# Key-value sums of a linear attention computed per image in column tiles, turned back by products with an identity, and the first loads and all engine orders rearranged

## The chip, the cores and the metric

The program runs on one core of one Trainium2 chip. The metric is device microseconds (us) of one execution. Each kernel is a single launch that takes the inputs of the reference, as float32, from HBM and writes the output back to HBM. Everything is computed in float32.

## The reference

The input is 8 images of 48 channels and 48 x 48 pixels. Two layers follow each other. The first is window attention (8 x 8 windows, 4 heads), a gated 1x1 convolution, a 3 x 3 convolution and a residual. The second is a depthwise block with linear attention and an MLP. The part that the change rewrites is the linear attention of the second layer:

```python
qk = t @ qk_w.T + qk_b                       # t: (b, n, 48) tokens, n = 2304
q = elu(qk[..., :c]) + 1.0
k = elu(qk[..., c:]) + 1.0
q_rope, k_rope = rope(q), rope(k)            # pairs of channels turned by the position
z = 1.0 / (einsum('bhnd,bhmd->bhnm', qh, k.mean(n)) + 1e-6)
kv = einsum('bhnd,bhne->bhde', k_rope * scale, v * scale)     # 8x8 per head, summed over n
attn = einsum('bhnd,bhde->bhne', q_rope, kv) * z
```

In the first layer the queries and keys are `x @ qkv_w.T + qkv_b`, and their biases are also touched.

## The kernel before, in words

The 8 images are worked on as 4 pairs (i = 0..3). Each pair is cut into 3 chunks of 16 image rows (n = 0..2), 768 pixels of each image. A tile has the 48 channels of one image on partitions 0 to 47 and those of the other on 64 to 111.

A job such as `kv.2.1` is one step of pair 2, chunk 1. Each engine has a table (`PE_ORDER`, `ACT_ORDER`, `DVE_ORDER`, `POOL_ORDER`, `SP_ORDER`) that lists its jobs in the order in which it issues them, and it never leaves that order. Jobs wait on semaphores. A PE job also names one of four PSUM slots (`@0` to `@3`); the slot must have been read by its previous user. Pair i+1's first layer is interleaved with pair i's second layer, so that only the second layer of pair 3 stands alone at the end.

Jobs that the prediction speaks of, first layer: `q1`, `k1` (queries, keys; L646), `qb` (DVE) and `kx` (ACT, L953) read them out, `xw` (ACT, L944) regroups pixels into windows, `v` (values, L703), `sc0..3` (scores, L718), `sb0..3` (DVE: add the bias, take the maximum, L1186 and L1190), `su` (POOL: subtract it), `ex` (ACT: exp, L974), `tr0..3` (transposes, L729), `pt` (ACT), `sm` (sums, L739), `av`, `pj`, `w1a`, `w1b`, `g`, and `cv` (the 3 x 3 convolution, 36 matmuls, L656 with `G`).

Second layer: `d0` (depthwise convolution as 36 matmuls, L656 with `ZP`), `ip`, `c10..c18` (DVE: nine taps of a depthwise convolution, L1230 and L1234), `ts`, `q`, `kt`, `vt` (queries, keys, values; L814, L804, L821), `c20..c28` (DVE: nine taps, L1245 and L1248), `kr`, `qs`, `qc` (POOL: rotations), and then the steps that change:

- `kv` (L829, L835): for each of the 8 token tiles of a chunk (98 rows: 96 tokens and a gap of two), keys (98 x 96, both images) are the weights, and a column of ones or the values (98 x 96) stream. The rotated keys come as two tiles, `KC` (times cosine) and `KS` (times sine). The result has keys of both images against values of both images; only the two diagonal blocks are used.
- `ks` (DVE, L1273, L1275) adds the three chunks of a pair in `kv_sum`.
- `kp` (L844 to L847) brings `kv_sum` into the layout with 64 partitions per image with matrices `wide_sb` (an identity and a swap of neighbouring channels); DVE `kp` scales it and cuts it to the heads (L1281, L1283), into `kv_sb` and `km_sb`.
- `kk` (L853) multiplies `kv_sb` by the swap matrix; DVE `kk` copies that to `kv2_sb` (L1289).
- `dn` (L862: the denominators, needs `kp`), `at` (L875: needs `kp`, `kk`, `qs`, `qc`), `az`, `am` (DVE), `ym` (POOL, L1393), `op` (L637), `oz` (DVE), `d3` (a second depthwise convolution, L656), `xc2`, `va2`, `f10..f12`, `f2`.

Before the first job, DVE and POOL clear tiles; SP and ACT issue the loads of weights. PE starts with a wait for all 30 loads of the group `loaded_a` (`pe.wait_ge(loaded_a, N_A * 16)`, L898). The last loads, 49 of `loaded_b`, are issued ahead of SP's order, whose first entry is `lx.0.2`, the load of the third chunk of pair 0.

Of the kernel before, what the change touches and what calls it, by code (L numbers as in the profile page):

```python
# [26 lines left out]
CH = 3  # L27
# [42 lines left out]
    cv.0.1@3 k1.1.1@0 cv.0.2@2 q1.1.1@1 d0.0.0@0 d0.0.1@1 xc.0.0@0 sc0.1.1@2 xc.0.1@1 tr1.1.0@3 va.0.0@0 va.0.1@1  # L70
    d0.0.2@3 tr2.1.0@2 ip.0.0@0 sc1.1.1@3 ip.0.1@1 v.1.0@0 tr3.1.0@1 sc2.1.1@3 sc3.1.1@0 xc.0.2@2 va.0.2@2 sm.1.0@1
    tr0.1.1@3 ip.0.2@2 q1.1.2@1 tr1.1.1@3 k1.1.2@2 ac.0.0@0 v.1.1@3 sc0.1.2@1 av.1.0@2 tr2.1.1@0 tr3.1.1@1 sc1.1.2@3
    ac.0.1@2 vt.0.0@0 sc2.1.2@1 pj.1.0@2 sm.1.1@0 q.0.0@3 tr0.1.2@2 sc3.1.2@0 w1b.1.0@1 kt.0.0@2 av.1.1@0 tr1.1.2@3
    k1.2.0@1 q1.2.0@2 pj.1.1@0 q.0.1@3 kt.0.1@2 v.1.2@0 tr3.1.2@3 tr2.1.2@2 sc0.2.0@1 w1a.1.0@3 sm.1.2@2 sc1.2.0@0
    kv.0.0@1 sc2.2.0@2 tr0.2.0@0 vt.0.1@3 av.1.2@0 sc3.2.0@3 q1.2.1@2 w1b.1.1@1 kt.0.2@0 pj.1.2@2 v.2.0@1 tr1.2.0@3
    k1.2.1@2 kv.0.1@0 q.0.2@3 vt.0.2@2 sc0.2.1@1 ac.0.2@0 kv.0.2@2 tr2.2.0@3 kp.0.0@2 sc1.2.1@3 tr3.2.0@0 dn.0.0@2
    dn.0.1@1 w1a.1.1@0 sm.2.0@3 kk.0.0@0 sc2.2.1@2 at.0.0@0 dn.0.2@1 w1b.1.2@3 cv.1.0@2 at.0.1@1 tr0.2.1@0 w1a.1.2@2
    av.2.0@3 sc3.2.1@0 cv.1.1@2 op.0.0@0 v.2.1@2 tr1.2.1@3 op.0.1@1 q1.2.2@0 pj.2.0@2 k1.2.2@3 d3.0.0@1 at.0.2@0
    tr2.2.1@1 xc2.0.0@3 sc0.2.2@2 tr3.2.1@1 va2.0.0@3 w1b.2.0@0 cv.1.2@1 f10.0.0@0 op.0.2@2 f11.0.0@3 f12.0.0@0
# [1443 lines left out]
```

## Time and profile before

| | |
|---|---|
| median of 3 runs | 820.52 us (816.24 to 821.81) |
| profiled execution, its own time | 821.09 us |
| span of the profiled execution | 819.3 us |
| PE busy | 700.7 us, 86% |
| DVE busy | 536.2 us, 65% |
| ACT busy | 428.2 us, 52% |
| POOL busy | 299.6 us, 37% |
| mean granted TensorE clock | 0.906 |

The span runs from the first to the last instruction; the execution's own time is 1.8 us longer. Busy times overlap between the engines, so they don't add up to the span. Float32 matmuls appear as two records each in the trace, so that 8 matmuls read x16.

### The profile page before, as it was taken

Reading aid. Unit: us, or ns where it says so; the run is one execution under the profiler, and the core shown is the slowest. Engines: PE = TensorE matmul, PEld = TensorE weight load, DVE = VectorE, ACT = ScalarE, POOL = GpSimd, SP = SyncE. Lnnn points to the kernel's source line nnn. Section 1 sums busy time; section 2 is a strip of 40 time slices with the busy share of each in tenths; the row PEclk is TensorE's granted clock in tenths of the full one; section 3 lists DMA queues with packets and bytes.
Section 4 is the critical chain, followed back from the end, with each engine's and each line's share of the span. In section 5 each row is a group of like instructions: output and inputs, shape, how many; then the busy total and the mean of one; then the engine's idle time right before and its main releaser. Section 6 shows DMA issues by size and latency. Waiting matters only on the chain. (4 is left out here: it accounts for less than half of the span.)

```text
span 819.3 us, 20532 instructions
## 1 busy us (share of the span) xinstructions
PE 700.7 (86%) x8964; PEld 416.1 (51%) x8964; DVE 536.2 (65%) x569; ACT 428.2 (52%) x521; POOL 299.6 (37%) x197
## 2 busy tenths in 40 slices
PE   1979989689896999989898999879789997686895
...
PEclk9999999889898999999889999876799998595799
...
GB/s 60 54 45 32 16 47 31 44 2 30 31 2 16 16 17 69 51 30 32 1 16 2 2 61 45 60 1 2 1 1 3 31 61 43 1 2 0 1 2 44
DMA packets 20395, 20.57 MB, mean 25 GB/s; under 512 B 9712, under 2 KB 19056, under 8 KB 20306
## 3 DMA queue, kind: packets, MB, share of 16 engines
...
q10 hardware_dynamic: 2080, 0.29, 0.2%
...
## 5 line engine op out<-in xcount | busy, mean ns | idle before, releaser
L656 PE MATMUL ps<-ZP,wdw 48*64 48x384 f32 x1728 | 148.3, 495 | 7.5 <-DVE ZP L1303 5.1
L1374 POOL TENSOR_TENSOR SC<-SC,mx 128x768 f32<-128x768 f32 x48 | 82.5, 1720 | 197.1 <-DVE mx L1190 196.9
L1248 DVE SCALAR_TENSOR_TENSOR CT<-TP,vec_sb,CT 112x768 f32<-112x768 f32 x96 | 146.8, 1539 | 1.8
L1234 DVE SCALAR_TENSOR_TENSOR QS<-ZP,vec_sb,QS 112x768 f32<-112x768 f32 x96 | 113.8, 1192 | 2.3
L656 PEld LDWEIGHTS ps<-ZP,wdw 48*64 48x64 f32 x1728 | 74.3, 136 | 78.0 <-issue 37.2
L1186 DVE TENSOR_TENSOR SC<-ps,bias_sb 128x768 f32<-128x768 f32 x48 | 45.7, 952 | 65.9 <-PE ps L718 32.0
L656 PE MATMUL ps<-G,w_sb 48*64 48x384 f32 x864 | 76.2, 501 | 6.5 <-ACT G L1007 6.2
L1220 DVE TENSOR_TENSOR LV<-LV,XB 112x768 f32<-112x768 f32 x24 | 25.9, 1081 | 72.5 <-ACT LV L1039 72.5
L935 ACT ACT_TABLE_LOAD x56 | 71.8, 1283 | 1.0
L656 PEld LDWEIGHTS ps<-G,w_sb 48*64 48x64 f32 x864 | 38.9, 138 | 41.1 <-issue 16.3
L729 PE MATMUL ps<-ident_sb,SC 128*128 128x128 f32 x288 | 48.1, 316 | 5.8 <-ACT AR L1051 2.6
L982 ACT ACTIVATE PT<-ps 128x768 f32<-128x768 f32 x48 | 38.1, 807 | 25.2 <-issue 12.7
L1345 POOL TENSOR_TENSOR KC<-KK,rope_th_sb 98x384 f32<-98x384 f32 x12 | 17.3, 1440 | 90.2 <-DVE KK L1254 90.1
L646 PE MATMUL ps<-XR,wt_sb 49*64 49x384 f32 x192 | 26.9, 644 | 26.4 <-DMA bv_sb<-in_vec_dram 18.0
L729 PEld LDWEIGHTS ps<-ident_sb,SC 128*128 128x128 f32 x288 | 37.4, 161 | 22.1 <-issue 19.3
L974 ACT ACTIVATE SC<-SC 128x768 f32<-128x768 f32 x48 | 39.7, 838 | 16.0 <-POOL SC L1374 15.8
L718 PE MATMUL ps<-kx,qw 32*64 32x128 f32 x1152 | 45.4, 302 | 1.9 <-DVE qw L1177 1.0
L1381 POOL TENSOR_TENSOR YF<-X1T,YF 112x768 f32<-112x768 f32 x12 | 21.3, 1778 | 69.7 <-ACT YF L1016 69.7
L1190 DVE TENSOR_REDUCE mx<-SC 128x12 f32<-128x768 f32 x48 | 45.7, 953 | 1.7
L1393 POOL TENSOR_TENSOR CT<-CT,AR 112x768 f32<-112x768 f32 x12 | 22.4, 1871 | 62.0 <-DVE CT L1298 62.0
L718 PEld LDWEIGHTS ps<-kx,qw 32*64 32x64 f32 x1152 | 34.1, 146 | 16.4 <-issue 11.6
L1090 ACT ACTIVATE QH<-ps,fc1b 128x768 f32<-128x768 f32 x36 | 30.5, 899 | 18.8 <-PE ps L646 18.7
...
## 6 DMA issues: line engine op xcount, KB each, us to landing
...
XR<-in_x_dram SPq DMA_DIRECT2D x24, 144.0 KB, 2.7
X1T<-in_x_dram SPq DMA_DIRECT2D x24, 144.0 KB, 2.9
...
out_dram<-XB SPq DMA_DIRECT2D x24, 144.0 KB, 2.3
...
```

Source lines behind the costliest of these rows:

```text
L656: mm = pe.matmul(slot(job)[half(c, HALF), r * BANK:r * BANK + SPX], w[half(r), tap * HALF:(tap + 1) * HALF], shifted(t, d * CROWS + c * WI ...
L718: mm = pe.matmul(slot(job)[half(c, HALF), p * BANK + wp * 128:p * BANK + (wp + 1) * 128] .rearrange("p (h y x) -> p h y x", h=2, y=WIN), q ...
L729: mm = pe.transpose(slot(job)[:, j * 128:(j + 1) * 128], SC[q % NSC][:, j * 128:(j + 1) * 128], ident_sb[:, :])
L935: act.preload_act_table_set(TABLE[name, i, n])
L974: act.activation(SC[q % NSC], SC[q % NSC], ACT.Exp).then_inc(exp_ready, 1)
L982: act.activation(PT[q % NPT], slot(job)[:, 0:CPX], ACT.Copy).then_inc(free(job), 2)
L1090: act.activation(pairs(HB[:, m, :]), two(job, 128), ACT.Gelu, bias=fc1b2[:, m:m + 1])\
L1186: dve.tensor_tensor(sc, two(job, 128).rearrange("p b (j m) -> p b j m", m=TOK), bias_sb[:, :].unsqueeze(1).unsqueeze(1).broadcast_to([128, ...
L1190: dve.tensor_reduce(mx[:, (q % NSC) * 12:(q % NSC) * 12 + 12], SC[q % NSC].rearrange("p (j m) -> p j m", m=TOK), AX.X, ALU.max)\
L1234: dve.scalar_tensor_tensor(out=rows16(T0[n]), in0=win, scalar=wt, in1=rows16(T0[n]), op0=ALU.mult, op1=ALU.add).then_inc(dwc_step, 1)
L1248: dve.scalar_tensor_tensor(out=ct, in0=win, scalar=wt, in1=ct, op0=ALU.mult, op1=ALU.add).then_inc(lepe_step, 1)
L1374: pool.tensor_tensor(sc, sc, bc_last(mx[:, (q % NSC) * 12:(q % NSC) * 12 + 12], TOK), ALU.subtract).then_inc(sub_ready, 1)
```

## The change

What is computed stays the same. The parts are:

1. **Key-value sums.** In `kv` the values are now the weights and the rotated keys stream, one image at a time: 98 x 48 weights, 48 streamed columns, image 0 into PSUM partitions 0 to 47 and image 1 into 64 to 111. The products of the two images are issued in turn, and there is nothing of image 0 against image 1 any more. A chunk has 16 + 32 matmuls where it had 8 + 16, each with half the weight columns and half the streamed columns (the means stream 2 as before).
2. **Turning back.** `ks` adds 112 x 96 and 112 x 2. With the third chunk, four more small DVE operations (112 x 24) combine the cosine and sine sums into `kv_turn`. `kp` transposes it by products with an identity: 12 matmuls of 48 rows and 64 columns. DVE `kp` has three operations where it had four. `kk` is gone from PE and DVE, and so are `swap_sb`, `wide_sb` and their ten loads.
3. **First-layer biases.** The query and key biases are no longer a 49th row of the weights (eight loads of 24 elements); they are added when DVE and ACT read the products out, from `vq_sb` and `kb_sb`.
4. **First loads.** The four loads of query and key weights come first on SP and have a semaphore of their own (`loaded_q`), for which PE waits at its start. The other 18 of `loaded_a` are waited for by `s1`, `v.0.0`, the first `tr`, and by DVE, which makes `kb_sb`. `lx.0.2` is issued before the last weights. `w2` has its own semaphore. Clearing of `vx`, `YF` and `XA` moves from DVE to POOL.
5. **Orders.** All five tables are new.

```diff
 PE_ORDER = """
-    k1.0.0@0 q1.0.0@1 s1.0.0@2 sc0.0.0@0 sc1.0.0@2 sc2.0.0@1 v.0.0@3 sc3.0.0@0 k1.0.1@2 q1.0.1@3 tr0.0.0@1 sc0.0.1@2
...
+    k1.0.0@0 q1.0.0@1 s1.0.0@2 v.0.0@3 sc0.0.0@0 sc2.0.0@2 sc1.0.0@3 sc3.0.0@1 k1.0.1@0 q1.0.1@3 tr0.0.0@0 tr1.0.0@2
...
-        N_A, N_B, N_W = 30, 49, 6
+        N_A, N_B, N_W, N_Q, N_C = 18, 37, 6, 4, 2
...
+            sp.wait_ge(zeroed, 1)
+            load(0, 0)
...
+            run("lx", 0, 2)
             load_turned(0, 1)
             load_turned(0, 2)
...
                 elif name in ("q1", "k1"):
                     pe.wait_ge(x_loaded[n], i * 32 + 32)
-                    turned(job, w4("q" if name == "q1" else "k", slice(0, K1)), XR[(i * CH + n) % 2], C + 1)
+                    turned(job, w4("q" if name == "q1" else "k", slice(0, K1)), XR[(i * CH + n) % 2])
...
                     for t in range(CT_):
-                        pe.matmul(ps[0:R, R:R + 2], KK[n % 2][:, t * R:(t + 1) * R], ones2,
-                                  start=(t == 0), stop=(t == CT_ - 1))
+                        for b in range(2):
+                            at = t * R + b * C
+                            pe.matmul(ps[half(b), BANK:BANK + 2], KK[n % 2][:, at:at + C], ones2,
+                                      start=(t == 0), stop=(t == CT_ - 1))
                     wait_read(pe, ("vt", i, n))
                     pe.wait_ge(kcs_ready, KR_COUNT["kr", i, n] * 4)
-                    for src, at in ((KC, 0), (KS, BANK)):
-                        for t in range(CT_):
-                            mm = pe.matmul(ps[0:R, at:at + R], src[n % 2][:, t * R:(t + 1) * R],
-                                           VT[:, t * R:(t + 1) * R], start=(t == 0), stop=(t == CT_ - 1))
+                    for t in range(CT_):
+                        for src, to in ((KC, 0), (KS, C)):
+                            for b in range(2):
+                                at = t * R + b * C
+                                mm = pe.matmul(ps[half(b), to:to + C], VT[:, at:at + C], src[n % 2][:, at:at + C],
+                                               start=(t == 0 and src is KC), stop=(t == CT_ - 1 and src is KS))
...
-                elif name == "kk":
-                    wait_read(pe, ("kp", i, 0))
-                    wait_slot(pe, job)
-                    pe.matmul(slot(job)[0:RG, 0:2 * HALF], swap_sb[:, :], kv_sb[:, :], start=True, stop=True)\
-                        .then_inc(fill(job), 1)
...
-            pe.wait_ge(loaded_a, N_A * 16)
+            pe.wait_ge(loaded_q, N_Q * 16)
...
+                    if n == CH - 1:
+                        wait_read(dve, job)
+                        even = lambda t, at: t[:, at:at + C].rearrange("p (c u) -> p u c", u=2)[:, 0]
+                        odd = lambda t, at: t[:, at:at + C].rearrange("p (c u) -> p u c", u=2)[:, 1]
+                        dve.tensor_tensor(even(kv_turn, 0), even(kv_sum, 0), odd(kv_sum, C), ALU.subtract)
+                        dve.tensor_tensor(odd(kv_turn, 0), odd(kv_sum, 0), even(kv_sum, C), ALU.add)
+                        dve.tensor_tensor(even(kv_turn, HALF), odd(kv_sum, 0), even(kv_sum, C), ALU.add)
+                        dve.tensor_tensor(odd(kv_turn, HALF), odd(kv_sum, C), even(kv_sum, 0), ALU.subtract)\
+                           .then_inc(kv_turned, 1)
```

**The head on SP.** The first loads as SP issues them, before:

```order
L500 DMA XR<-in_x_dram 48x768 x2
L512 DMA wt_sb<-in_wsq_dram 48x2x24 x4
L512 DMA wt_sb<-in_vec_dram 1x24x1 x8
L512 DMA wproj_sb<-in_wproj_dram 24x48
L512 DMA bv_sb<-in_vec_dram 24x1
```

(three more pairs of `wproj_sb` and `bv_sb` follow, and then the second `XR`.) With the change:

```order
L501 DMA wt_sb<-in_wsq_dram 48x2x24 x4
L498 DMA XR<-in_x_dram 48x768 x2
L516 DMA vq_sb<-in_vec_dram 24x20 x4
L498 DMA XR<-in_x_dram 48x768 x2
L516 DMA wproj_sb<-in_wproj_dram 24x48 x4
L512 DMA X1T<-in_x_dram 48x2x384 x2
L507 DMA wt_sb<-in_wsq_dram 48x2x48 x2
L507 DMA wt_sb<-in_vec_dram 1x48x1 x4
L498 DMA XR<-in_x_dram 48x768 x2
```

The eight loads of bias elements are gone, and the third `XR` load (`lx.0.2`), which stood behind all weights, is now ahead of the last `X1T` loads.

**PE at the end of pair 2's attention**, where `G` marks the convolutions `cv.3.n` of pair 3 and `ZP` the convolutions `d3.2.n` of pair 2. Before, from the last output product of pair 2 (`op.2.2`, L637) to the first convolution of pair 3's second layer (`d0.3.0`, the last row):

```order
L637 MATMUL ps<-CT,wsq_sb 112x384 x2
L646 MATMUL ps<-LV,wln_sb 64x384 x4
L656 MATMUL ps<-ZP,wdw 64x384 x36
L646 MATMUL ps<-LV,wfc_sb 64x384 x8
L646 MATMUL ps<-XB,wln_sb 64x384 x4
L656 MATMUL ps<-ZP,wdw 64x384 x36
L646 MATMUL ps<-LV,wfc_sb 64x384 x4
L646 MATMUL ps<-LV,wln_sb 64x384 x4
L646 MATMUL ps<-XB,wln_sb 64x384 x4
L656 MATMUL ps<-G,w_sb 64x384 x36
L646 MATMUL ps<-LV,wln_sb 64x384 x4
L892 MATMUL ps<-QH,wfc_sb 64x384 x12
```

With the change, the stretch between the first `dn` of pair 2 (L871) and that output product has all three `G` convolutions:

```order
L871 MATMUL ps<-QH,km_sb 64x384 x4
L658 MATMUL ps<-G,w_sb 64x384 x36
L871 MATMUL ps<-QH,km_sb 64x384 x4
L884 MATMUL ps<-QH,kv_sb 64x384 x4
L884 MATMUL ps<-QS,kv_sb 64x384 x4
L658 MATMUL ps<-G,w_sb 64x384 x36
L871 MATMUL ps<-QH,km_sb 64x384 x4
L884 MATMUL ps<-QH,kv_sb 64x384 x4
L884 MATMUL ps<-QS,kv_sb 64x384 x4
L639 MATMUL ps<-CT,wsq_sb 112x384 x2
L658 MATMUL ps<-G,w_sb 64x384 x36
L639 MATMUL ps<-CT,wsq_sb 112x384 x2
```

So `cv.3.2` no longer stands between pair 2's output product and `d0.3.0`.

**DVE at the start of pair 2's taps.** `SC` and `mx` are the last softmax step of pair 3 (`sb3.3.2`), `QS` the taps `c1x.2.n`, `CT` the taps `c2x.2.n`. With the change:

```order
L1196 TENSOR_TENSOR SC<-ps,bias_sb 128x768
L1200 TENSOR_REDUCE mx<-SC 128x12
L1240 TENSOR_SCALAR QS<-ZP,vec_sb 112x768
L1244 SCALAR_TENSOR_TENSOR QS<-ZP,vec_sb,QS 112x768 x2
L1207 TENSOR_TENSOR NI<-ps,NI 128x768
L1244 SCALAR_TENSOR_TENSOR QS<-ZP,vec_sb,QS 112x768
```

Before, that softmax step stood behind all 27 `QS` taps and the first `CT` taps. Now it stands ahead of them; the other first-layer steps of pair 3 (`nm`, `x1`, `g`) stay between the taps.

## Rows read from the trace of the kernel before

**Rows 1.** The page: PE's busy time, and the granted clock in 40 slices.
```profile
PE 700.7 (86%) x8964; PEld 416.1 (51%) x8964; DVE 536.2 (65%) x569; ACT 428.2 (52%) x521; POOL 299.6 (37%) x197
...
PEclk9999999889898999999889999876799998595799
```
**Rows 2.** Stretches: from:to, us, busy PE, PEld, DVE, ACT, POOL (instructions), granted clock, DMA, GB/s.
```profile
55.00:519.00 464.00, 428.78 (x6142) 255.06 (x6142) 312.94 (x337) 272.59 (x340) 175.65 (x103) 0.94 0.09 26
519.00:627.00 108.00, 89.39 (x1014) 57.56 (x1010) 92.00 (x88) 51.26 (x63) 47.12 (x28) 0.81 0.04 12
627.00:658.00 31.00, 30.36 (x360) 16.00 (x355) 4.82 (x5) 16.53 (x18) 4.68 (x3) 1.00 0.08 21
...
697.00:753.00 56.00, 39.24 (x294) 30.32 (x294) 54.32 (x54) 26.26 (x27) 34.10 (x20) 0.68 0.00 1
```
**Rows 3.** Waits of PE: us in total, times, longest.
```profile
PE ps L656 <- ACT G L1007: 6.2, 1, 6.2
```
**Rows 4.** Timeline of the head: start, us, engine, line, operation, [idle before]; q: DMA issue.
```profile
0.74 0.31 POOL L1319 MEMSET wt_sb<- 113x256 f32 x1 [0.29 <-POOLq L1513]
...
5.27 0.43 ACTq L908 DMA_DIRECT2D masks_sb<-in_masks_dram  x1
5.29 1.87 SPq L512 DMA_DIRECT2D wt_sb<-in_wsq_dram  x4
...
7.20 6.19 SPq L512 DMA_DIRECT2D wt_sb<-in_vec_dram  x8
...
12.72 0.73 ACTq L908 DMA_DIRECT2D wide_sb<-in_const_dram  x1
...
18.02 2.84 PE L646 MATMUL ps<-XR,wt_sb 49*64 49x384 f32 x16 [18.02 <-DMA bv_sb<-in_vec_dram]
...
19.65 1.69 ACT L953 ACTIVATE kx<-ps,hmask_sb 128x768 f32<-128x768 f32 x2 [4.89 <-PE ps L646]
...
21.23 0.93 ACT L944 ACTIVATE XW<-XR 112x384 f32<-112x384 f32 x2
...
29.24 1.28 ACT L935 ACT_TABLE_LOAD   x1
...
32.06 1.54 PE L729 MATMUL ps<-ident_sb,SC 128*128 128x128 f32 x6
...
48.60 2.84 PE L646 MATMUL ps<-XR,wt_sb 49*64 49x384 f32 x16 [4.64 <-DMA XR<-in_x_dram]
...
52.84 2.53 PE L739 MATMUL ps<-PT,ones_sb 128*32 128x384 f32 x16
```
**Rows 5.** The page's DMA issues: count, KB, median us from issue to landing.
```profile
XR<-in_x_dram SPq DMA_DIRECT2D x24, 144.0 KB, 2.7
```
**Rows 6.** Timeline of PE: one chunk of `kv` and what follows it, pair 0.
```profile
196.63 1.52 PE L829 MATMUL ps<-masks_sb,KK 98*96 98x2 f32 x16
198.01 1.58 PE L835 MATMUL ps<-VT,KC 98*96 98x96 f32 x16
...
200.88 0.89 PE L718 MATMUL ps<-kx,qw 32*64 32x128 f32 x24
```
**Rows 7.** Timeline of PE: the value products of pair 0, chunk 1.
```profile
60.08 1.60 PE L703 MATMUL ps<-wv_sb,XW 112*64 112x48 f32 x48
```
**Rows 8.** Timeline of DVE: two of its steps between the taps of pair 2.
```profile
570.91 0.96 DVE L1186 TENSOR_TENSOR SC<-ps,bias_sb 128x768 f32<-128x768 f32 x1 [0.89 <-PE ps L718]
...
594.63 0.29 DVE L1289 COPY kv_sb<-ps 112x128 f32<-112x128 f32 x1 [2.52 <-PE ps L853]
```
**Rows 9.** Timeline of PE: the last convolution of pair 3's first layer.
```profile
647.39 6.02 PE L656 MATMUL ps<-G,w_sb 48*64 48x384 f32 x72
```
**Rows 10.** Timeline of DVE in the last pair: six taps in a row.
```profile
727.98 11.74 DVE L1248 SCALAR_TENSOR_TENSOR CT<-TP,vec_sb,CT 112x768 f32<-112x768 f32 x6
```
**Rows 11.** Timeline of PE in the last pair: `kp` and `dn`.
```profile
740.94 0.58 PE L844 MATMUL ps<-kv_sum,wide_sb 96*112 96x48 f32 x2 [5.74 <-DVE kv_sum L1275]
...
744.13 1.56 PE L862 MATMUL ps<-QH,km_sb 48*64 48x384 f32 x8 [0.82 <-DVE kv_sb L1283]
```

More of the change, by code:

```diff
@@ L70 @@
[L70 to L79, printed above, removed]
@@ new lines @@
+    g.1.2 sb0.2.1 c25.0.1 sb1.2.1 ks.0.2 sb2.2.1 kp.0.0 sb3.2.1 qb.2.2 c24.0.0 c25.0.0 c26.0.1 c26.0.0 nm.2.0 c27.0.0
+    az.0.0 c28.0.0 az.0.1 c27.0.1 am.0.0 sb0.2.2 c28.0.1 x1.2.0 am.0.1 c20.0.2 c21.0.2 oz.0.0 c22.0.2 oz.0.1 c23.0.2
+    c24.0.2 c25.0.2 c26.0.2 c27.0.2 az.0.2 c28.0.2 am.0.2 g.2.0 oz.0.2 sb1.2.2 yn2.0.0 sb2.2.2 sb3.2.2 nm.2.1 yn2.0.1
+    o.0.0 qb.3.0 yn2.0.2 sb0.3.0 sb1.3.0 o.0.1 yn.1.0 o.0.2 sb2.3.0 yn.1.1 x1.2.1 c10.1.0 c11.1.0 c12.1.0 sb3.3.0
+    c13.1.0 qb.3.1 c14.1.0 yn.1.2 c15.1.0 nm.2.2 c16.1.0 g.2.1 c17.1.0 c10.1.1 c18.1.0 c10.1.2 c11.1.1 x1.2.2 c12.1.1
@@ new lines @@
+    c11.1.2 c13.1.1 c12.1.2 qo.1.0 c13.1.2 c14.1.1 ko.1.0 c15.1.1 c14.1.2 c16.1.1 c15.1.2 c17.1.1 c16.1.2 c18.1.1
+    c17.1.2 sb0.3.1 c18.1.2 ks.1.0 sb1.3.1 c20.1.0 ko.1.1 c20.1.1 g.2.2 c21.1.1 c21.1.0 c22.1.1 ko.1.2 c22.1.0 c23.1.1
+    c23.1.0 qo.1.1 c24.1.0 ks.1.1 c25.1.0 ks.1.2 qo.1.2 c26.1.0 nm.3.0 kp.1.0 c27.1.0 c24.1.1 c28.1.0 c25.1.1 sb2.3.1
+    az.1.0 am.1.0 c26.1.1 x1.3.0 c27.1.1 az.1.1 c28.1.1 am.1.1 oz.1.0 c20.1.2 c21.1.2 c22.1.2 oz.1.1 c23.1.2 az.1.2
+    c24.1.2 c25.1.2 c26.1.2 c27.1.2 c28.1.2 am.1.2 sb3.3.1 oz.1.2 qb.3.2 yn2.1.0 g.3.0 sb0.3.2 sb1.3.2 yn2.1.1 o.1.0
@@ L575, in _ @@
                 for m in range(2):
-                    load_a(wt4_g[half(b), m, :, 0:hh_],
+                    load_q(wt4_g[half(b), m, :, 0:hh_],
                            wsq3[img, m, img].rearrange("r (g c) -> r g c", g=2))
-            bias_row(load_a, "bq", "q")
-            bias_row(load_a, "bk", "k")
+            sp.wait_ge(zeroed, 1)
+            load(0, 0)
+            sp.wait_ge(setup_pool, 2)
+            for b in range(2):
+                for g in range(2):
+                    rows = slice(b * HALF + g * QUAD, b * HALF + g * QUAD + hh_)
+                    load_a(vq_sb[rows, :], vec[g * hh_:(g + 1) * hh_, 0:VI["bv"] + 1])
+            sp.wait_ge(zeroed, 2)
+            load(0, 1)
             for b in range(2):
@@ L917, in _ @@
                     load_a(hmask_sb[row:row + C // 2, :], masks[g * (C // 2):(g + 1) * (C // 2), 2 + 2 * g:4 + 2 * g])
[L918 to L920 removed]
+            for b in range(2):
+                load_a(wv_sb[half(b), :], wsq[b * C:(b + 1) * C, 2 * R:3 * R])
+            load_a(bias_sb[:, :], bias)
+            load_a(ident_sb[:, :], ident)
+            for b in range(2):
+                load_a(vec_sb[half(b), :], vec[b * C:(b + 1) * C, :])
+            act.wait_ge(setup_pool, 3)
             load_b(masks_sb[:, :], masks)
@@ L1324, in _ @@
             op_.then_inc(setup_pool, 1)
+            pool.memset(vx, 0.0).then_inc(setup_pool, 1)
+            for j in range(2):
+                op_ = pool.memset(YF[j], 0.0)
+            op_.then_inc(setup_pool, 1)
+            pool.memset(XA[:, :], 0.0)
             pool.memset(ZP[:, :, :], 0.0)
```

348 lines of the change are left out of this document (173 added, 175 removed).

## The prediction

> **What bounds the kernel now.** I read the page's busy times first. PE is busy 700.7 us of 819.3, more than any other engine, at a granted clock that is mostly full and falls in a few slices [rows 1]. Then the busy time by stretch [rows 2] shows three regimes. From 55 to 519 us PE is busy 92% (428.8 of 464) at clock 0.94: here PE work removed is time removed. From 519 to 627, pair 2's taps, DVE is busy 92.0 of 108 us, PE 89.4 at clock 0.81: DVE's order sets the pace, and PE waits in between. From 627 to 658 PE alone works (30.4 of 31, DVE 4.8). From 697 to 753, in the lone pair 3, DVE is busy 54.3 of 56 and PE's clock is 0.68. Ahead of all that lies a head in which PE stands 18.02 us for the first loads and once more 4.64 us for a third `XR` load [rows 4]. So a change is worth its PE time in the first regime, its DVE time in the second and last, and its start in the head.
>
> **The sum, against the profiled execution's own 821.1 us.**
>
> *Head.* POOL's first clearing ends at 0.74 + 0.31 = 1.05. The four weight loads (1.87) then end their issue at 3.0, the `XR` load (as the six of pair 0, 0.9) at 3.9, and it lands 2.7 later [rows 4, 5]: PE starts near 6.8, where it started at 18.02. Eight bias loads of 6.19 us are gone. PE can't use all of it. ACT issues 5 loads after its first ten, not 13; those 13 took 5.27 to 13.45, 0.63 each, and the ten took from 0.74 to 5.27, so ACT is free at 1.4 + 4.5 + 3.2 = 9.1 (the 1.4 is POOL's second group of clearings, an estimate from its first). Then follow a table load 1.28, `xw` 0.93 and `kx` 1.69 [rows 4]: `v` starts at 11.3. PE is at its low clock here (a transpose takes 1.54), so I give `v` twice the 1.60 of its full-clock row, less overlap, 2.9, four score steps 1.5 each, like the transpose, and the next key product half of 2.84: to 21.6 [rows 4, 7]. ACT runs the second `kx` *before* the first `ex`, so 1.7, a table load of 1.3 and one activation (half of `kx`'s pair, 0.85) pass before the first transpose: about 25.5, against 32.06 [rows 4]. That is 6.5 less. From there to the first `sm`, PE took 20.8 us, 4.64 of them the wait for `XR`, which now stands ahead of the late weights. The same PE work lies in between. So `sm.0.0` comes at 41.7, not 52.84, 11.1 less. Of this I take **-10.2**, because DVE runs `sb1` before `sb2` where PE runs `sc2` first, which can cost one of these steps. Bounds: -6.5 if the `XR` wait comes back, -15 if ACT's late loads don't hold it.
>
> *Key-value sums.* A chunk took from 196.63 to 200.88, 4.25 us for 48 records, 88 ns each, with 2 streamed columns as with 96 [rows 6]. Now there are 96 records in two column halves. The nearest row is `v`: weights of 112 x 64 in two column halves, 48 columns streamed, 48 records in 1.60 us, 33 ns each [rows 7]. 96 x 33 ns = 3.2 us, 1.07 less per chunk. `kp` and `kk` had 14 records (2.4 us at the low clock in the last pair up to `dn` with their DVE part 3.2 [rows 11], about half of the PE part at full clock, 1.2, and 0.6 for `kk`); 24 records at 33 ns are 0.8, 1.0 less. In the PE-bound regime there are six chunks and two `kp`: 6 x 1.07 + 2 x 1.0 = **-8.4**. Pair 2's three chunks lie beside DVE's taps, pair 3's under 54.3 us of DVE in 56: nothing there for themselves. The bounds: 88 ns per record as before would make a chunk 8.4 us, +4.2; half of `v`'s time would make it 1.6, -2.7.
>
> The Trainium skill (TensorE: Matmul & The Clock Gate, Back-to-back issue gap) has an issue floor of about 25 ns for small matmuls; an estimate by that page is 96 x 25 = 2.4 us per chunk, which would make the sum 5 us lower. No run here shows that floor for these shapes, and the row for `v` is above it.
>
> *Pair 2 beside the taps.* `sb3.3.2` (0.96 + 0.95) leaves the taps' stretch for the PE-bound one before it. The `kk` copy goes, and the 2.52 us for which DVE stood before it [rows 8]; 0.5 us of new small DVE operations come (estimate: four of about 0.12). DVE had 16 us idle in this stretch, so some of this may only move: **-4.2**, between 0 and -12.
>
> *`cv.3.2`.* It was one of the jobs of 627 to 658, where PE alone works: 6.02 us [rows 9]. It moves in among pair 2's `at` and `op`, where PE idles 18.6 of 108 us. The work between `op.2.2` and `d0.3.0` falls by its 5.8 us of pace: **-5.8**. Price if the cover is gone: it delays `at.2.1` or `op.2.1` by up to 5.8, and the gain is nil.
>
> *Last pair.* `ks.3.2` and `kp` come after 9 `CT` taps instead of 11, at 11.74 / 6 = 1.96 us each [rows 10], while `kv.3.2` is ready: -3.9. `kp` to `dn` took 3.2 us [rows 11]; four DVE operations of some 0.1, 24 short records and three DVE operations give 2.2: -1.0. But DVE now runs tap `c28.3.2` after `az.3.2`, on the chain to the last `op`: +1.0. Together **-3.9**, between 0 and -8. What is late next there is POOL, whose `qc.3.0` and `qc.3.1` start with `dn`.
>
> *Orders.* In pairs 0 and 1, the 6.2 us wait of `cv.1.1` for its edges [rows 3] should go: 24 us of PE work now lie between `w1a.1.2` and it. Against that, `pj.2.2` now stands right behind `av.2.2`, `w1b.1.1` right behind `pj.1.1`, and `vt` right ahead of `kv` in pair 1. I put this at **0**. PE idles 35 us in 55 to 519 [rows 2], so new waits could bring +17 (half as much again), or -12 (a third less).
>
> Sum: -10.2 - 8.4 - 4.2 - 5.8 - 3.9 = -32.5, so 788.6 for the execution's own time. The median of the three runs shown is 0.6 us under that of the profiled one: **788 us**.
>
> **The rivals.**
>
> *A. The order's own waits (805 us).* Each term above assumes that no other wait takes its place. With +17 from 55 to 519 us the sum is 805.6 and the median 805. For it: DVE is already busy 313 of 464 us there, and `sb3.3.2` and parts of pair 3's softmax are now in it. Against it: the distances in PE work between producer and consumer are mostly as long as before.
>
> *B. The head is swallowed (798 us).* If the first convolutions wait for weights or the `YF` path, the 10.2 is lost. Against it: PE is busy nearly throughout from 55 us on, and the late weights are issued earlier too.
>
> *C. The column halves don't run side by side (830 us, slower).* The place is `kv`: both halves use all 98 rows, and stream different columns. If each record costs 88 ns as before, a chunk costs 8.4 us: +4.2 on each of six chunks (25), instead of -6.4, and about +8 in pairs 2 and 3 where PE has room for the rest: 788.6 + 6.4 + 25 + 8 = 828, and with `kp` 830. It decides from 44 ns per record on: above that `kv` is dearer than before. Against it: `v` has the same form and runs at 33 ns [rows 7].
>
> The Trainium skill (TensorE: Matmul & The Clock Gate, What overlaps and what doesn't) says that a weight load overlaps running matmuls only when its row group differs. By that rule the two halves, which share all rows, would come one after the other. The row for `v` disagrees, since its halves share 112 rows.
>
> *D. More than the sum (776 us).* With three convolutions in the waits of pair 2, PE's clock, 0.81 there, stays full, and 12 of DVE's 16 idle us go.
>
> **How the numbers follow.** Chances: forecast 0.58, A 0.20, B 0.07, C 0.05, D 0.10. The predicted time is the forecast's. The range is 774 to 808: it takes in the forecast, B, D and most of A, and leaves out C and A's far end. About 1% (8 us) is what a measurement can tell from no change. Faster by more than that (under 812) are all cases but C and a tail of A: 0.89. Within 1%: 0.06. Slower: 0.05.
>
> **What would show it.** PE's first record near 7 us, the first transpose near 26, the first `sm` near 42. A `kv` chunk of 96 records in 3.2 us at full clock. `d0.3.0` 27 to 30 us earlier than 657.7, and its distance to the end 3 to 5 us shorter. No wait of 6 us for `G`. Wrong it would be if a chunk takes over 4.2 us, if PE idles clearly more than 35 us between the first `sm` and pair 2's taps, or if DVE idles as long as before among pair 2's taps.

## The result and the profile after

The changed kernel took **796.75 us** (median of 4 runs, 794.74 to 800.78) against 820.52 before: a ratio of 0.9725, 95% interval 0.9668 to 0.9782. A second set of runs gave 799.63 and 0.9711 (0.9645 to 0.9777). The profiled execution took 800.78, the second set's 799.63. Now and then a kernel runs at a lower clock and takes 1.5% or more longer; medians and ranges in this document count such runs, ratios and their intervals leave them out. The forecast was 788, the range 774 to 808: faster as forecast, but 9 us short of it.

Page of the kernel after, busy times and granted clock in 40 slices (before: [rows 1]):

```profile
PE 684.9 (86%) x9580; PEld 380.8 (48%) x9580; DVE 528.7 (66%) x575; ACT 432.6 (54%) x523; POOL 316.6 (40%) x200
...
PEclk9999999989889999986869989978899997575899
```

PE has 16 us less busy time, but its mean clock went from 0.906 to 0.891. The busy time by stretch, cut where [rows 2] is, moved along with the jobs (columns as there):

```profile
42.00:505.00 463.00, 431.06 (x6492) 243.91 (x6492) 309.83 (x341) 278.74 (x351) 180.15 (x102) 0.92 0.11 28
505.00:598.00 93.00, 76.25 (x1154) 43.40 (x1150) 87.46 (x85) 46.08 (x54) 53.81 (x29) 0.87 0.02 5
598.00:632.00 34.00, 28.57 (x304) 13.40 (x296) 9.52 (x10) 15.34 (x17) 3.48 (x2) 0.95 0.07 19
677.00:733.00 56.00, 34.30 (x464) 23.70 (x464) 51.50 (x52) 21.57 (x23) 37.91 (x21) 0.62 0.01 1
```

The first stretch is almost as long as before (463 against 464 us), though six key-value chunks in it are shorter. The taps' stretch went from 108 to 93 us, with DVE idle 5.5 us instead of 16. The last one, the lone pair, has a clock of 0.62.

The head, PE's timeline (start, us, line, operation, [idle before]), of the kernel after:

```profile
6.87 2.84 PE L648 MATMUL ps<-XR,wt_sb 48*64 48x384 f32 x16 [6.87 <-DMA XR<-in_x_dram]
...
12.27 2.81 PE L708 MATMUL ps<-wv_sb,XW 112*64 112x48 f32 x48 [0.91 <-ACT XW L951]
...
25.32 2.79 PE L736 MATMUL ps<-ident_sb,SC 128*128 128x128 f32 x12 [2.91 <-ACT SC L983]
...
40.20 1.86 PE L746 MATMUL ps<-PT,ones_sb 128*32 128x384 f32 x16
```

This answers to [rows 4]: PE starts at 6.87, the 4.64 us wait for the third `XR` load is gone, and `sm.0.0` comes at 40.20 instead of 52.84.

Where the time came from, by jobs that both kernels have (us; "again" is the second profile of the same kernel):

| stretch | before | after | again | forecast of the difference |
|---|---|---|---|---|
| to `d0.0.0` | 112.1 | 99.1 | 99.3 | -10.2 |
| `d0.0.0` to `d0.2.0` (pairs 0, 1) | 373.0 | 376.8 | 370.2 | -8.4 |
| `d0.2.0` to `d0.3.0` (pair 2) | 172.7 | 158.4 | 161.2 | -10.0 |
| `d0.3.0` to `f2.3.2` (pair 3) | 155.1 | 158.3 | 160.6 | -3.9 |

The head and pair 2 gave more than forecast. Pairs 0 and 1 gave 3 us at most where 8 were forecast, pair 3 took time, and that is where the 9 us lie.

### The profile page after: what moved, and what is told of

Same layout as the page of the kernel before. It is cut to its first block, busy times and chain, and to the rows that moved or that the text cites. A ratio compares the mean times of both kernels' runs of the same rounds, so it can differ in the third digit from the quotient of the medians.

```text
span 799.0 us, 21754 instructions
## 1 busy us (share of the span) xinstructions
PE 684.9 (86%) x9580; PEld 380.8 (48%) x9580; DVE 528.7 (66%) x575; ACT 432.6 (54%) x523; POOL 316.6 (40%) x200
## 4 chain that ended last, share of the span: by engine, by line
PE 30%; DVE 13%; issue 5%; ACT 5%; POOL 3%; DMA 1%; SPq 0%; ACTq 0%; DVEq 0%
PE ps L658 13%; PE ps L648 6%; DVE CT L1258 5%; DVE QS L1244 4%; PE ps L902 2%; PE ps L811 2%; PE ps L884 2%; PE ps L639 1%; ACT L942 1%; PE ps L846 1%; PE ps L821 1%; POOL QH L1387 1%; PE ps L736 1%; PE ps L723 1%; ACT LV L1046 1%
## 5 line engine op out<-in xcount | busy, mean ns | idle before, releaser
L1400 POOL TENSOR_TENSOR SC<-SC,mx 128x768 f32<-128x768 f32 x48 | 80.6, 1680 | 214.2 <-DVE mx L1200 214.0
L1258 DVE SCALAR_TENSOR_TENSOR CT<-TP,vec_sb,CT 112x768 f32<-112x768 f32 x96 | 151.1, 1591 | 0.9
L1244 DVE SCALAR_TENSOR_TENSOR QS<-ZP,vec_sb,QS 112x768 f32<-112x768 f32 x96 | 107.2, 1160 | 0.3
L658 PE MATMUL ps<-G,w_sb 48*64 48x384 f32 x864 | 79.0, 520 | 0.1
L1371 POOL TENSOR_TENSOR KC<-KK,rope_th_sb 98x384 f32<-98x384 f32 x12 | 17.6, 1466 | 98.6 <-DVE KK L1264 98.5
L658 PEld LDWEIGHTS ps<-G,w_sb 48*64 48x64 f32 x864 | 35.2, 144 | 42.8 <-issue 40.6
L723 PE MATMUL ps<-kx,qw 32*64 32x128 f32 x1152 | 47.3, 313 | 1.1 <-ACT kx L962 0.8
L736 PEld LDWEIGHTS ps<-ident_sb,SC 128*128 128x128 f32 x288 | 35.9, 157 | 25.3 <-issue 21.3
L983 ACT ACTIVATE SC<-SC 128x768 f32<-128x768 f32 x48 | 39.5, 837 | 13.9 <-POOL SC L1400 13.7
L723 PEld LDWEIGHTS ps<-kx,qw 32*64 32x64 f32 x1152 | 35.7, 153 | 18.7 <-issue 14.4
L1037 ACT ACTIVATE XB<-ps,vec_sb 112x768 f32<-112x768 f32 x12 | 10.8, 900 | 56.8 <-PE ps L658 56.8
L1419 POOL TENSOR_TENSOR CT<-CT,AR 112x768 f32<-112x768 f32 x12 | 25.0, 2079 | 41.5 <-DVE CT L1319 41.5
```

Source lines behind the costliest of these rows:

```text
L658: mm = pe.matmul(slot(job)[half(c, HALF), r * BANK:r * BANK + SPX], w[half(r), tap * HALF:(tap + 1) * HALF], shifted(t, d * CROWS + c * WI ...
L723: mm = pe.matmul(slot(job)[half(c, HALF), p * BANK + wp * 128:p * BANK + (wp + 1) * 128] .rearrange("p (h y x) -> p h y x", h=2, y=WIN), q ...
L736: mm = pe.transpose(slot(job)[:, j * 128:(j + 1) * 128], SC[q % NSC][:, j * 128:(j + 1) * 128], ident_sb[:, :])
L983: act.activation(SC[q % NSC], SC[q % NSC], ACT.Exp).then_inc(exp_ready, 1)
L1244: dve.scalar_tensor_tensor(out=rows16(T0[n]), in0=win, scalar=wt, in1=rows16(T0[n]), op0=ALU.mult, op1=ALU.add).then_inc(dwc_step, 1)
L1258: dve.scalar_tensor_tensor(out=ct, in0=win, scalar=wt, in1=ct, op0=ALU.mult, op1=ALU.add).then_inc(lepe_step, 1)
```

## The experiments

Two theories: **orders**, the new tables cost in pairs 0 and 1 what the shorter key-value sums save; and **code**, the short matmuls themselves, or chance in the clock, do it. "Low" below is time at the lower granted clock (1.2 GHz).

### The same kernel again

> The changed kernel once more. The order theory (the new orders themselves leave PE at its low clock between d0.1.0 and d0.2.0) expects the same picture again: 795 to 800 us, some 186 us from d0.1.0 to d0.2.0, of which 45 to 65 us at the low granted clock. The chance theory (that stretch was a mishap of the one profiled execution, whose 800.8 us was the longest of four) expects under 35 us at the low clock there and a length of 170 to 176 us.

799.63 us (792.38 to 812.95), ratio 0.9711 (0.9645 to 0.9777). From `d0.1.0` to `d0.2.0`: 180.6 us, 41 of them low (first profile: 186.5 and 55; before: 166.9 and 17). So the stretch is long and low each time, as the order theory said (with 4 us less low time than its 45 to 65), but its length moves by 6 us between two executions. No effect of a few us inside one stretch can be read from one profile.

### Code without the new orders

```diff
-PE_ORDER, ACT_ORDER, DVE_ORDER, POOL_ORDER, SP_ORDER: new
+the tables of the kernel before, without kk
```

> The changed code and first loads with the orders of the kernel before (kk taken out of two tables). By the terms of the prediction: head -10, key-value sums -8.4, last pair -1, so 801 us. With a key-value chunk at the measured 2.4 us instead of 3.2: 796 us. The order theory expects d0.1.0 to d0.2.0 in 165 us or less with about 17 us at the low clock, as in the kernel before. If instead the short key-value matmuls bring the clock down, that stretch is 175 us or more with over 40 us at the low clock, and the time is above 803 us.

807.6 us (802.04 to 811.3), ratio 0.9881 (0.982 to 0.9941). `d0.0.0` comes at 98.6, 13.5 us earlier than before; everything behind it is as long as before (374.3, 171.5, 155.4). All of the gain is the head. The forecast of 796 to 801, which counted the key-value sums, was missed. From `d0.1.0` to `d0.2.0` it took 168.9 us with 27 low. That is close to the kernel before (166.9 and 17) and far from the changed one, so most of the long stretch is not the code's doing; but the total is above 803, as the code theory expected.

### New orders without the code

```diff
+kk.i.0 behind dn.i.0 on PE, behind kp.i.0 and two more jobs on DVE (code of the kernel before)
```

> The code of the kernel before with the new orders (the swap product kk behind the first dn of each pair, its DVE copy two taps behind kp). By the prediction's terms for orders: pair 2 -3.7, cv.3.2 -5.8, last pair -2.9, the wait for G -6 at most, kk kept +0: 806 to 810 us. The order theory expects 180 us or more from d0.1.0 to d0.2.0 with over 40 us at the low clock, and a total of 810 to 816. The theory that the short matmuls do it expects under 172 us and under 25 us at the low clock there.

The profiled run took 820.54, that of before 821.09; the other three took 833.1 to 839.4, which leaves one run to compare. None of the four is faster than the kernel before, where 806 to 816 was expected. In the profile pairs 0 and 1 take 379.6 instead of 373.0, pair 2 161.4 instead of 172.7, pair 3 161.4 instead of 155.1. From `d0.1.0` to `d0.2.0` it took 184.2 us with 34 low. So the long stretch comes with the orders, without any short matmul. The low time is under the 40 us that were expected.

### Key-value sums alone

```diff
+kv, ks, kp, at of the change; kk gone (head and orders of the kernel before)
```

> Only the key-value sums of the change (kv, ks, kp, at; kk gone) in the kernel before, with its head and its orders. By the prediction's term: -8.4 -1 = 811 us. With 2.4 us per chunk and 0.8 per kp: 6 x 1.9 + 2 x 1.6 + 1 = -15.6, 805 us. If what PE saves there turns into waits for DVE: 817 us or more. Rival C of the prediction (halves one after the other) expects 828 us.

820.76 us (815.18 to 825.3, 10 runs), ratio 1.0037 (1.0002 to 1.0073): no gain at all. Of what was expected only "817 us or more" held. A chunk took 2.36 us, half of before, and still nothing. The place where it is lost, PE's timeline around the second and third chunk of pair 0, of the kernel before:

```profile
220.88 1.52 PE L835 MATMUL ps<-VT,KS 98*96 98x96 f32 x16
222.34 0.88 PE L814 MATMUL ps<-TP,wlq_sb 49*64 49x384 f32 x8
223.14 0.97 PE L821 MATMUL ps<-ident_sb,TP 112*98 112x112 f32 x8
224.05 0.89 PE L718 MATMUL ps<-kx,qw 32*64 32x128 f32 x24
225.44 0.88 PE L646 MATMUL ps<-LV,wt_sb 48*64 48x384 f32 x8 [0.51 <-DVE kv_sum L1275]
```

and of the kernel with the sums alone:

```profile
217.88 0.26 PE L840 MATMUL ps<-KS,VT 98*48 98x48 f32 x4
219.02 0.88 PE L815 MATMUL ps<-TP,wlq_sb 49*64 49x384 f32 x8 [0.88 <-ACT PT L986]
219.83 0.97 PE L822 MATMUL ps<-ident_sb,TP 112*98 112x112 f32 x8
220.73 0.88 PE L719 MATMUL ps<-kx,qw 32*64 32x128 f32 x24
222.98 1.20 PE L647 MATMUL ps<-LV,wt_sb 48*64 48x384 f32 x8 [1.37 <-DVE kv_sum L1281]
224.11 1.45 PE L832 MATMUL ps<-masks_sb,KK 98*48 98x2 f32 x32
225.41 0.38 PE L840 MATMUL ps<-KC,VT 98*48 98x48 f32 x4
```

DVE's timeline shows what the second of the two waits was for, before:

```profile
219.50 5.45 DVE L1248 SCALAR_TENSOR_TENSOR CT<-TP,vec_sb,CT 112x768 f32<-112x768 f32 x3
224.88 0.41 DVE L1275 TENSOR_TENSOR kv_sum<-ps,kv_sum 96x98 f32<-96x98 f32 x2
```

and with the sums alone:

```profile
217.14 5.46 DVE L1252 SCALAR_TENSOR_TENSOR CT<-TP,vec_sb,CT 112x768 f32<-112x768 f32 x3
222.52 0.31 DVE L1281 TENSOR_TENSOR kv_sum<-ps,kv_sum 112x96 f32<-112x96 f32 x2
```

Of the 1.95 us saved in the chunk, 0.88 turn into a wait for ACT that wasn't there, and 0.86 into a longer wait for DVE. Counted from the start of the chunk (218.09 and 215.77), both come as late as before: ACT's `PT` after 2.3 us and DVE's `kv_sum`, behind three taps, after 6.8. Then PE's clock falls (the product `ac.0.2` takes 1.20 instead of 0.88, a step of four records 0.38 instead of 0.26), and the next chunk takes 4.08 us. The pair's first chunk had started 2.3 us earlier than in the kernel before and the job behind it 4.0 us, but `kp.0.0` starts only 1.6 us earlier.

The profiled run, 815.18, is the fastest of the ten. Their mean granted clock is 0.872 to 0.899, that of 13 runs of the kernel before 0.900 to 0.918: the clock is lower in every one of them, not only in the profile.

### The sums computed twice

```diff
-                    for t in range(CT_):
+                    for t in [t for rep in range(2) for t in range(CT_)]:
```

> The kernel with only the key-value sums changed (old head, old orders), with the 64 records... of each chunk's rotated part issued twice (128 of 160 records; same result), so that a chunk takes 96 + 64 records at 25 ns = 4.0 us, about the 4.3 us of the kernel before. It tells why the granted clock fell at ac.0.2, 113.5 us behind d0.0.0, where the kernel before held it. If the short matmuls themselves bring the clock down: it falls there again, with a chunk kv.0.2 of 6 to 8 us. If it is PE standing still because it is ahead of its partners (gaps of 0.88 and 1.37 us before q.0.2 and ac.0.2): those gaps go back under 0.6 us, the clock stays full there, and d0.0.0 to d0.2.0 takes 371 to 376 us though PE does 13 us more work than with single matmuls.

814.61 us (809.73 to 815.75, 10 runs), ratio 0.9956 (0.9924 to 0.9988): *faster* than with the sums once, by 0.8% of before, with intervals that don't touch. The wait before `q.0.2` is gone, that before `ac.0.2` (1.31 us) stayed, and behind it the clock fell again, so this place does not tell whether the short matmuls or the standing PE bring the clock down. The whole stretch tells what PE's work is worth. From the first chunk to `d0.2.0`, in turn before, sums once, sums twice (us, busy PE, PEld, DVE, ACT, POOL, clock):

```profile
196.60:485.00 288.40, 265.60 (x3578) 159.52 (x3578) 212.23 (x206) 158.32 (x194) 128.36 (x74) 0.95 0.08 24
```

```profile
194.40:484.10 289.70, 259.88 (x3887) 150.49 (x3887) 214.82 (x210) 158.62 (x194) 127.18 (x74) 0.92 0.09 24
```

```profile
190.35:480.70 290.35, 263.84 (x4271) 158.93 (x4271) 214.10 (x210) 158.57 (x194) 128.06 (x74) 0.93 0.08 24
```

The six chunks need 26 us before, 14 with the sums once and 23 with them twice (4.32, 2.36, 3.81 each at full clock), and the stretch is 288 to 290 us in all three. **In these profiles PE work in this stage has no worth in the old orders, in either direction**, though PE was busy 92% of it before. The 4 us by which the profile with doubled sums is ahead of the other arise between `d0.0.0` and the first chunk, where both kernels are the same, out of less low time (10 against 20 us). The ten runs keep that advantage, and their clocks go with it: 0.907 to 0.918, against 0.872 to 0.899 with the sums once. What lowers the clock there is open.

### Fewer taps on DVE, without and with the new sums

```diff
+                        if k == 4 and i < 2:
+                            win, ct = win[:, 0:1, 0:8], ct[:, 0:1, 0:8]
```

> The kernel before, with one tap (c24) of each chunk of pairs 0 and 1 cut to 8 elements: 6 x 1.96 = 11.8 us of DVE work left out (that tap's products are missing). The bound theory of the prediction (PE, busy 92%, sets the pace there) expects no gain: 817 to 820 us. The lockstep theory (each engine waits for the other in turn, so that neither alone gives its whole saving) expects 3 to 7 us: 812 to 815. If DVE is the bound: 808 us or less.

> The kernel with only the key-value sums changed, and the same taps left out in pairs 0 and 1. If DVE's work is what took back PE's saving of some 13 us in pairs 0 and 1, d0.0.0 to d0.2.0 falls from 374 to 362 us or less, and the total is 803 to 808 us. If the saving was taken back by something else (ACT, POOL, the clock), that stretch stays at 370 us or more and the total at 813 to 817.

815.37 us (ratio 0.9969, 0.9928 to 1.001) and 814.66 (0.9965, 0.9925 to 1.0004). The edit left out less than it was meant to. The 1.96 us per tap come from the last pair; in pairs 0 and 1 the six taps took 8.6 us before and 3.9 with the edit, so that 4.7 us went, not 11.8, and the bounds that were expected for DVE don't apply. In the kernel before, leaving them out is worth less than can be told. With the sums alone it is worth about 6 us (820.76 to 814.66, intervals that just touch), as much as DVE's busy time fell (539.1 to 532.6). With the taps out, PE's shorter sums are worth 0.7 us.

From the first chunk to `d0.2.0` the first took 283.8 us with 24 low, the second 290.6 with 58 low. These two profiles are the second fastest and the second slowest of their ten runs, so most of that difference is the execution's. PE's idle time from `d0.0.0` to `d0.2.0` fell by only 1.5 and 1.8 us through the edit (31.8 to 30.3, 38.8 to 37.0). So DVE's work alone doesn't explain where PE's saving goes, but that DVE sets the pace in places, as around `kv_sum` above, isn't ruled out.

### New head and orders with the old sums

```diff
-kv, ks, kp, at of the change
+those of the kernel before, kk as in the test of the orders
```

> The changed kernel with the key-value sums of before (kv, ks, kp, kk, at as they were; their loads last on SP), so the new head and the new orders alone. If the short matmuls are worth what the prediction gave them (-8.4 and -1.0): 806 to 809 us. If they are worth nothing, as alone in the old orders: 797 to 800 us. From d0.0.0 to d0.2.0 the first expects 8 us more than the 377 and 370 us of the changed kernel's two profiles, the second the same.

812.73 us (805.83 to 828.25, 10 runs), ratio 0.9914 (0.9869 to 0.996), against 0.9711 (0.9645 to 0.9777) with the new sums. The difference of the two ratios is 2.0%, against the first set's 0.9725 it is 1.9%. **In the new orders the sums are worth some 16 us** (10 to 23 by the two intervals), more than the 9.4 forecast; in the old ones nothing. Both expectations for this run were missed, since both gave it a shorter time. Pairs 0 and 1 took 381.3 us, pair 2 163.8, pair 3 165.0: 5 to 11, 3 to 5 and 4 to 7 us more than the two profiles of the changed kernel. A caution: where `kk` stands in these orders was my choice, and its own waits are in these numbers.

### The old order in the last pair

```diff
-PE, ACT, DVE behind f2.2.2, x3.3.1, o.2.2: new
+the order of the kernel before
```

> The changed kernel, but from the first convolution of pair 3's second layer on, PE, ACT and DVE follow the orders of before. In the changed kernel d0.3.0 to f2.3.2 took 158 and 161 us, in the kernel before 155, and with only the code changed 155. If the new order of the taps is what costs there: 153 to 156 us for that stretch and 793 to 795 us in all. If it is the state in which the stretch starts, or the clock: 158 to 161 us and 797 to 800 us.

798.96 us (794.85 to 803.55): no difference in all. The stretch took 156.9 us. It is shorter behind `dn.3.0` (68.8 us to `f2.3.2` instead of 73.6 and 74.1) and longer ahead of it (88.1 from `d0.3.0` instead of 84.7 and 86.5). So the new order gains 2 to 3 us up to `dn.3.0` and loses 5 behind.

### The column halves one after the other

```diff
-                    for t in range(CT_):
-                        for src, to in ((KC, 0), (KS, C)):
-                            for b in range(2):
+                    for b in range(2):
+                        for t in range(CT_):
+                            for src, to in ((KC, 0), (KS, C)):
```

> The changed kernel with the rotated part of each chunk issued image by image (all 16 products of image 0, in one column half, then all of image 1) instead of in turn. If 25 ns per record comes from the two column halves running side by side, a chunk takes 32 + 64 records at about 45 to 50 ns for the latter, 3.7 to 4.0 us at full clock instead of 2.36. If 25 ns is a floor of issue that any record of this size meets, it stays at 2.36 to 2.45 us.

One run, 803.52 us. PE's timeline in a chunk of the changed kernel (L838 the means, L846 the sums):

```profile
209.46 0.89 PE L838 MATMUL ps<-masks_sb,KK 98*48 98x2 f32 x32
210.19 0.28 PE L846 MATMUL ps<-KC,VT 98*48 98x48 f32 x4
210.30 0.26 PE L846 MATMUL ps<-KS,VT 98*48 98x48 f32 x4
210.39 0.26 PE L846 MATMUL ps<-KC,VT 98*48 98x48 f32 x4
```

and of this one:

```profile
209.47 0.89 PE L838 MATMUL ps<-masks_sb,KK 98*48 98x2 f32 x32
210.21 0.27 PE L846 MATMUL ps<-KC,VT 98*48 98x48 f32 x2
210.32 0.25 PE L846 MATMUL ps<-KS,VT 98*48 98x48 f32 x2
210.41 0.25 PE L846 MATMUL ps<-KC,VT 98*48 98x48 f32 x2
```

A row starts every 0.09 us in both, with four records in the one and two in the other: 22 and 45 ns per record. A chunk took 3.66 us instead of 2.36. The halves do run side by side, over the same 98 rows, and 25 ns is not a pace that any record of this size keeps.

### The first transpose without its wait

```diff
 ACT_ORDER
-    xw.0.0 kx.0.0 vx.0.0 kx.0.1 ex0.0.0
+    xw.0.0 kx.0.0 vx.0.0 ex0.0.0 kx.0.1
 PE_ORDER: slots 0 and 2 exchanged from tr0.0.0 on
```

> The changed kernel with ACT's first ex ahead of the second kx, and PE's slots 0 and 2 exchanged from the first transpose on, so that it waits for that ex alone. The wait of 2.9 us ahead of the first transpose should fall to 0.5 to 1.5 us, and the first transposes start at 23.5 to 24 instead of 25.3. The second still waits for both, so sm.0.0 comes 0 to 1.5 us earlier, and the total does not move by what can be told: 796 to 799 us.

789.78 us (two runs, 789.05 and 790.5), ratio 0.9631 (0.9566 to 0.9697). It is the shortest of all kernels here, but its interval overlaps that of the changed kernel. PE's timeline:

```profile
19.42 2.84 PE L648 MATMUL ps<-XR,wt_sb 48*64 48x384 f32 x16
22.19 2.44 PE L736 MATMUL ps<-ident_sb,SC 128*128 128x128 f32 x12
...
32.40 1.50 PE L746 MATMUL ps<-PT,ones_sb 128*32 128x384 f32 x16
```

The wait is gone entirely, 3.1 us, and `sm.0.0` comes 7.8 us earlier, far more than forecast. The rest is the clock: it is full from 23.9 us on here, from 41.0 in the kernel after. Without the edit it came at 28.6 once (the kernel with old sums: `sm.0.0` at 35.9). The five other profiles of the changed kernel and its near variants have it at 39.8 to 43.9. Whether the missing wait brings it or chance is open.

### PE kept busy in the last pair

```diff
+            def keep_busy(job, count):
+                wait_slot(pe, job)
+                for j in range(count):
+                    for c in range(2):
+                        pe.matmul(slot(job)[half(c, HALF), 0:SPX], w2_sb[:, 0:HALF], w2_sb[:, HALF:HALF + SPX],
+                                  start=True, stop=True)
```

> The changed kernel with 23 pairs of idle matmuls (64 x 384, overwritten later) in nine of PE's waits in pair 3's second layer, some 17 us of work at full clock in about 28 us of waits. If the low clock there (68 and 75 us, of which 43 and 45 us busy) is what PE's standing still brings, and it is on the path: low-clock time under 45 us from d0.3.0 to f2.3.2, that stretch 148 to 155 us instead of 158 to 161, total 788 to 793. If DVE alone sets that stretch: clock up, but length 157 us or more, total as before. If the added matmuls only delay: 162 us or more.

800.26 us (791.07 to 806.64), as without. Its profiled run is the longest of the four, 806.64, so that its shares say more than its lengths. From `d0.3.0` on, first the kernel after, then this one:

```profile
634.30:798.00 163.70, 116.71 (x1288) 59.03 (x1284) 95.59 (x94) 72.06 (x78) 50.63 (x27) 0.79 0.07 17
```

```profile
639.60:804.00 164.40, 133.67 (x1380) 65.96 (x1376) 96.01 (x94) 72.10 (x78) 48.87 (x27) 0.84 0.07 17
```

17 us more busy, clock 0.84 instead of 0.79, the same length. The other three runs had a mean clock of 0.901 to 0.918 over the whole span, the first four of the changed kernel 0.890 to 0.897, and no less time. So a higher clock bought this way gains nothing. That the clock costs nothing there isn't shown: `op.3.2` came later than in the changed kernel (125.4 us behind `d0.3.0`, instead of 122.6 and 124.4), but took 1.54 us instead of 2.90, and from it to `f2.3.2` there were 33.4 us instead of 35.6 and 36.2. The added matmuls may have taken ahead of it what the clock gave behind.

## Why the prediction was right and where it failed

**Head: right, a little more.** -13.0 at `d0.0.0` against -10.2. The times on the way agree: 6.87 (near 7), `v` at 12.3 (11.3), the first transpose at 25.3 (25.5), `sm.0.0` at 40.2 (41.7). With the code but not the orders it is the whole gain. How much it gives varies with the execution: the six profiles with the head of before reach `d0.0.0` at 109.9 to 112.5, six with the new head at 98.1 to 99.3, and two whose clock was full earlier at 91.5 and 93.7.

**Key-value sums: the size of a chunk was off, and the step "PE work removed is time removed" failed.** A chunk takes 2.36 us, 25 ns per record, not 3.2; the kernel saves 1.95 us per chunk at full clock, not 1.07. The Trainium skill (TensorE: Matmul & The Clock Gate, Back-to-back issue gap) has an issue floor of about 25 ns, and the estimate of 2.4 us by it was the better one in number. Why is another matter: with the halves one after the other the same records took 45 ns each, and in turn 22. The Trainium skill's rule that a weight load overlaps running matmuls only where the row group differs (same page, What overlaps and what doesn't) is not what these rows show: two column halves over the same rows take half the time per record when issued in turn. Rival C was rightly given little.

But 92% busy did not mean that PE set the pace. This is the step that failed. PE's account from `d0.0.0` to `d0.2.0` shows what became of its saving (us; "work" is PE's busy time less half of that at the low clock, an estimate of the work at full clock; "clock" is that half; one profile each):

| kernel | length | work | idle | clock |
|---|---|---|---|---|
| before | 373.0 | 317.2 | 31.8 | 24.0 |
| sums alone | 374.2 | 303.7 | 38.8 | 31.7 |
| code without orders | 374.3 | 303.7 | 41.6 | 29.0 |
| sums twice | 370.7 | 312.8 | 35.5 | 22.4 |
| orders alone | 379.6 | 322.3 | 28.9 | 28.4 |
| new head and orders, old sums | 381.3 | 321.9 | 27.2 | 32.2 |
| changed kernel | 376.8 | 308.1 | 30.8 | 37.9 |
| changed kernel again | 370.2 | 308.3 | 31.1 | 30.8 |

In the old orders 13.5 us of work went, and 7 to 10 us of idle time and 5 to 8 us of low clock came. In the new orders 14 went and only 2 to 4 us of idle time came, with the low clock anywhere from 1 us less to 10 more. At the one place that was followed, PE's next job waits for ACT or DVE, which don't come earlier, and the clock falls behind the wait; that the wait brings the clock down isn't shown, since no test held the clock up in these pairs. The same code is worth some 16 us in orders that suit it. I had taken code and orders as terms to be added; they are not. In the old head each alone gave about 0. The head with the code gave -11, and with the orders too it is -19 to -24 us.

**Orders, put at 0: 7 to 8 us more in pairs 0 and 1** (379.6 and 381.3 with the old sums against 373.0). This is what ate the forecast -8.4, about half of rival A. But some 5 of them are PE work that now stands ahead of `d0.2.0` (322.3 and 321.9 against 317.2), most of it out of pair 2; the rest is the clock, while PE's idle time fell. Pair 0 gained 10.6 in the test of the orders, 6.2 of them the wait of `cv.1.1`, which went; pair 1 lost 17.3. Of those, 6 are work moved in (150.6 against 144.5), 3 idle, 8 the clock. The stretch in the kernel after, ahead of and in the longest low time of pair 1:

```profile
346.30:365.20 18.90, 14.11 (x213) 9.07 (x213) 16.68 (x13) 14.10 (x18) 11.28 (x6) 0.91 0.01 2
365.20:378.90 13.70, 12.68 (x133) 8.26 (x131) 12.05 (x16) 4.70 (x6) 6.25 (x5) 0.50 0.01 2
```

and the longest wait in it:

```profile
PE ps L648 <- DVE KK L1264: 2.4, 1, 2.4
```

PE was busy 14.1 of 18.9 us, and then worked 13.7 us at half clock. All eight profiles with the new orders have such a low time there, 13.7 to 23.9 us; the six with the old orders have at most 6.8 near it. My test for this rival, "PE idles clearly more than 35 us", could not see it: PE idled only 32 us from 42 to 505. The clock has to be read too.

**Pair 2 and `cv.3.2`: right, in part by luck.** -14.3 and -11.5 against -10.0, and -11.3 with the orders alone; DVE's idle time among the taps fell from 16 to 5.5 us, as meant. But 3.7 us of the -11.3 are PE work at full clock that moved into the pairs before (132.0 against 135.7), and the new code, whose PE work had been put at nothing here, gave 1.2 and 4.1 us in the two tests with the old orders.

**Last pair: wrong in sign**, +3 to +5.5 instead of -3.9. `kp.3.0` did come earlier relative to `d0.3.0`, by 2.7 us and by 0.8 in the second profile, where 3.9 were counted. Three things took that back. First, the four small DVE operations, put at 0.12 us each; no row gave that size. DVE's timeline of the kernel after, and POOL's beside it:

```profile
712.24 1.01 DVE L1292 TENSOR_TENSOR kv_turn<-kv_sum 112x24 f32<-112x24 f32 x1
713.17 0.17 DVE L1293 TENSOR_TENSOR kv_turn<-kv_sum 112x24 f32<-112x24 f32 x1
713.27 1.45 DVE L1294 TENSOR_TENSOR kv_turn<-kv_sum 112x24 f32<-112x24 f32 x1
714.64 0.17 DVE L1295 TENSOR_TENSOR kv_turn<-kv_sum 112x24 f32<-112x24 f32 x1
714.74 3.57 DVE L1258 SCALAR_TENSOR_TENSOR CT<-TP,vec_sb,CT 112x768 f32<-112x768 f32 x2
```

```profile
710.80 2.41 POOL L1387 TENSOR_TENSOR QS<-QS,rope_x_sb 112x768 f32<-112x768 f32 x1
713.17 1.51 POOL L1385 TENSOR_TENSOR QS<-QH,rope_y_sb 112x768 f32<-112x768 f32 x1
```

They take 2.6 us from first to last, not 0.5: the first ends as POOL's operation ends (713.25, 713.21), the third as POOL's next one does (714.72, 714.68). Second, DVE runs two taps, 3.57 us, before it reads `kp`, so `kp` to `dn` took 4.1 us instead of the 2.2 that I gave and the 3.2 of before. `at.3.0` then waits 3.7 us for POOL, which the prediction had named as late next. Third, one that I missed: `f12.3.0` now stands ahead of `op.3.2`:

```profile
755.42 1.56 PE L648 MATMUL ps<-LV,wfc_sb 48*64 48x384 f32 x8 [4.22 <-DVE LV L1230]
756.91 2.90 PE L639 MATMUL ps<-CT,wsq_sb 112*112 112x384 f32 x4
```

The 4.22 us wait uses up what was left of the lead: `op.3.2` starts 122.6 us behind `d0.3.0` in both kernels. Behind the wait it runs at the low clock, 2.90 us instead of 1.54, and from it to `f2.3.2` there are 35.6 and 36.2 us instead of 32.5. In all seven profiles with the old order of the tail this is 32.5 to 33.0, in those with the new one 35.0 to 36.2, or 33.4 where PE was kept busy. So it is the new order of the tail that costs there, and by the 33.4 a good part of it is the low clock.

**The whole: in the range, with luck in how it got there.** The head and pair 2 gave 4 to 7 us more than forecast, pairs 0 and 1 and the last pair 15 to 19 less. That it is faster was safe: the head and the stretch of pair 2 alone gave 24 to 27 us.
